# Memory attention with the rotary partner fetched by DMA between partitions

## The reference, cut to what matters

```python
qkv = xn @ w_qkv
q, k, v = jnp.split(qkv, 3, axis=-1)
rot = jnp.stack((-t2[..., 1], t2[..., 0]), axis=-1).reshape(t.shape)   # t2: t in pairs
roped = t * cos + rot * sin                                            # t: q and k
# per segment, with memory mem and norm z
sdpa = softmax(mask(roped_q @ roped_k.T * SCALE)) @ v
sq, sk = elu(q) + 1, elu(k) + 1
mem_out = (sq @ mem) / (sq @ z + 1e-6)
out = beta * mem_out + (1.0 - beta) * sdpa
prev_v = (sk @ mem) / (sk @ z)
mem = mem + sk.T @ (v - prev_v)
z = z + sk.sum(axis=2)
o = concat(out) @ w_out
```

## Time and profile before

| | |
|---|---|
| median of three runs | 2839.58 us |
| profiled execution, its own time | 2842.93 us |
| its span | 2840.8 us |
| TensorE busy in the whole span | 2095.6 us (74%) |
| VectorE | 1985.0 us (70%) |
| ScalarE | 1418.4 us (50%) |
| GpSimd | 1079.2 us (38%) |
| memory attention, about | 298 to 1130 us |
| its DMA traffic from 332 to 1130 us | 1 GB/s |

### The profile page before, as it was taken

The page is one execution under the profiler, slowest core; times in us unless marked ns, Lnnn a source line. Parts: engine busy times, 40 slices in busy tenths (PEclk is TensorE's granted clock), DMA queues, the critical chain, the costliest instruction groups (busy, mean ns, idle before and its releaser), DMA issues. The chain is left out here.

```text
span 2840.8 us, 87273 instructions
## 1 busy us (share of the span) xinstructions
PE 2095.6 (74%) x35326; PEld 1682.5 (59%) x35326; DVE 1985.0 (70%) x4767; ACT 1418.4 (50%) x2385; POOL 1079.2 (38%) x873
## 2 busy tenths in 40 slices
PE   3687599999999997679398947656666545558894
PEld 2576478888888876568278946433222233336794
DVE  5787577777777775779664433889999966757443
ACT  1555234444444442447364522468988754436452
POOL 3656334455554442556365621000000122206563
PEclk7789699999999998679699975765555577868997
DMA  4132200000000000023413220000000000012324
GB/s 109 45 103 83 80 2 0 0 0 0 0 0 0 0 0 3 31 83 93 147 45 91 73 88 0 0 0 1 1 0 0 0 1 1 0 36 70 88 77 114
DMA packets 95266, 104.00 MB, mean 37 GB/s; under 512 B 18936, under 2 KB 81000, under 8 KB 94464
## 3 DMA queue, kind: packets, MB, share of 16 engines
q1 hardware_dynamic: 74416, 64.12, 8.3%
q0 software_dynamic: 18176, 37.79, 3.9%
q10 hardware_dynamic: 2512, 0.02, 0.0%
HBM read 60.00 MB, written 46.20 MB: 37 GB/s over the span
## 5 line engine op out<-in xcount | busy, mean ns | idle before, releaser
L2472 POOL TENSOR_TENSOR bw_kT<-b_knT,b_head_of 128x768 f32<-128x768 f32 x40 | 58.5, 1494 | 650.7 <-SPq L2295 493.6
L2269 DVE CUSTOM_DVE_ANT_0 be_logs<-be_joint,be_logs 128x1024 f32<-128x1024 f32 x256 | 293.3, 1220 | 7.5 <-ACT be_logs L2242 7.5
L2242 ACT ACTIVATE be_logs<-be_joint,b_tiny 128x1024 f32<-128x1024 f32 x256 | 281.0, 1117 | 10.0 <-PE be_joint L2212 3.4
L2212 PE MATMUL be_joint<-be_partsT_k,be_partsT_q 64*128 64x512 f32 x512 | 195.4, 767 | 93.4 <-DVE be_sums L2269 89.9
L405 POOL DMA_INDIRECT d_pairs<-s_y_tile,s_x_tiles x156 | 178.6, 1145 | 119.4 <-DVE s_y_tile L1293 94.9
L1600 POOL TENSOR_TENSOR m_roped_q<-m_raw_q,m_cos 128x1024 f32<-128x1024 f32 x32 | 75.9, 2373 | 371.7 <-ACT m_raw_q L1536 371.7
L2212 PEld LDWEIGHTS be_joint<-be_partsT_k,be_partsT_q 64*128 64x128 f32 x512 | 72.0, 278 | 215.8 <-DVE be_sums L2269 211.3
L405 POOL DMA_INDIRECT d_pairs<-g_y_tile,g_x_tiles x156 | 153.9, 986 | 97.5 <-ACT g_y_tile L828 73.1
L332 POOL DMA_INDIRECT d_rows<-g_xn,g_slot x128 | 131.7, 1029 | 80.0 <-DVE g_slot L323 43.6
L332 POOL DMA_INDIRECT d_rows<-s_xn,s_slot x128 | 128.9, 1007 | 73.6 <-DVE s_slot L323 37.3
L1142 PE MATMUL s_ps_y<-s_down,s_a_tile 128*128 x1248 | 151.8, 275 | 0.0
(11 more groups left out here) (464 smaller groups left out, 6338.4 us busy)
## 6 DMA issues: line engine op xcount, KB each, us to landing
g_x_tiles<-d_rows SPq DMA_DIRECT2D x78, 132.0 KB, 2.1
s_x_tiles<-d_rows SPq DMA_DIRECT2D x78, 132.0 KB, 2.1
d_rows<-d_rows SPq DMA_DIRECT2D x32, 132.0 KB
g_shared<-d_pairs SPq DMA_DIRECT2D x8, 512.0 KB, 7.4
g_xn<-d_pairs SPq DMA_DIRECT2D x8, 512.0 KB, 7.5
s_up_raw<-L_ffn_We SPq DMA_DIRECT2D x16, 256.0 KB, 5.3
s_down<-L_ffn_We SPq DMA_DIRECT2D x16, 256.0 KB, 5.8
s_up_raw<-d_pairs SPq DMA_DIRECT2D x8, 512.0 KB, 7.5
```

What stands on the lines that cost most here:

```text
L2212: last = nc.tensor.matmul(joint_ps[k % DEPTH][:, a, :], partsT[0][rows, b, i * P:(i + 1) * P], partsT[1][rows, b, half * 512:(half + 1) * ...
L2242: nc.scalar.activation(logs[k % DEPTH][:, :, :], joint_ps[k % DEPTH][:, :, :], ACT.Ln, bias=A.tiny[:, :]).then_inc(s.log_ready, 1)
L2269: nc.vector.tensor_tensor_reduce(out=flat, in0=joint_ps[k % DEPTH][:, :, :].rearrange("p a j -> p (a j)"), in1=flat, scale=1.0, scalar=0.0 ...
L2472: last = nc.gpsimd.tensor_tensor(kT[:, h, :, :], A.knT[:, bass.ds(j * GROUP, KEYS), :], A.head_of[:, h:h + 1].unsqueeze(2).broadcast_to([P ...
```

## The change

The second set of fills goes, with `w_rot`. `front_spin` on VectorE now multiplies the same fill that gives `raw` by `signed_sin` (sin with the sign of the partition it is to leave from) into `spun`, after ScalarE has copied that half. SyncE then copies `spun` to `turned`, odd partitions to even ones and even to odd, in halves of 512 columns: eight transfers a tile, each of 64 partitions of 2 KB. GpSimd's products and sums are in halves too: all four products first, then the four sums, each of which waits for its transfers.

The orders change. k comes ahead of q everywhere. k's fills use banks 1 and 3 and q's banks 0 and 2; `project` uses bank 1 in place of a bank of `back_ps`. `scores(w)` moves from the end of tile `w - 1` to behind `recall_q` of tile `w`. VectorE begins a tile with `norm_1`, `back_u` and `back_o`, and the softmax follows in four parts around the two `back_mem`. Semaphores are split by q and k. The prologue fills k first, and TensorE no longer computes scores in it.

```diff
+            def swap(f, k):
+                spun_sem, moved, roped_sem = ((s.q_spun, s.q_moved, s.q_roped), (s.k_spun, s.k_moved, s.k_roped))[k]
+                for half in range(2):
+                    chunks = slice(4 * half, 4 * half + 4)
+                    wait_alone(sp, spun_sem, at(f, 2, half + 1), s.passed)
+                    wait(sp, roped_sem, at(f, 2, half - 1))
+                    sp.dma_start(turned[k][0::2, chunks, :], spun[k][1::2, chunks, :]).then_inc(moved[half], 16)
+                    sp.dma_start(turned[k][1::2, chunks, :], spun[k][0::2, chunks, :]).then_inc(moved[half], 16)
...
-            def fill_q(f, half):
-                if half == 0:
-                    pe.wait_ge(s.xnT_ready, f + 1)
+            def fill_k(f, half):
+                if half == 0:
+                    pe.wait_ge(s.xnT_ready, f + 1)
+                    wait(pe, s.scores_read, f)
+                fill(2 * half + 1, w_qkv, INNER + 512 * half, s.k_full)
+            def fill_q(f, half):
                 wait(pe, s.phik_copied, at(f, 2, half - 1))
                 fill(2 * half, w_qkv, 512 * half, s.q_full)
-                wait(pe, s.scores_read, f)
-                fill(2 * half + 1, w_rot, 512 * half, s.q_full)
...
             def recall_q(w, half):
-                wait_alone(pe, s.u_ready, at(w, 2, half + 1), s.passed)
+                if half == 0:
+                    pe.wait_ge(s.q_phi, w + 1)
+                wait_alone(pe, s.back_step, at(w, 8, 2 * half + 2), s.passed)
                 recall(phi_qT, half)
...
                 recall_q(w, 0)
-                if more:
-                    fill_q(w + 1, 0)
                 recall_q(w, 1)
-                if more:
-                    fill_q(w + 1, 1)
+                scores(w)
                 additions(w, 0)
                 if more:
                     fill_k(w + 1, 0)
+                    fill_k(w + 1, 1)
                 additions(w, 1)
                 if more:
-                    fill_k(w + 1, 1)
+                    fill_q(w + 1, 0)
+                    fill_q(w + 1, 1)
                 answers(w)
                 if more:
                     fill_v(w + 1)
-                project(w)
-                if more:
-                    scores(w + 1)
+                project(w, more)
...
+            def rope_moved(f, k):
+                cos_sem, moved, roped_sem = ((s.q_cos, s.q_moved, s.q_roped), (s.k_cos, s.k_moved, s.k_roped))[k]
+                for half in range(2):
+                    chunks = slice(4 * half, 4 * half + 4)
+                    pool.wait_ge(cos_sem, at(f, 2, half + 1))
+                    pool.wait_ge(moved[half], at(f, 32, 32))
+                    nc.gpsimd.tensor_tensor(roped[k][:, chunks, :], roped[k][:, chunks, :], turned[k][:, chunks, :], ALU.add).then_inc(roped_sem, 1)
...
+                for half in range(2):
+                    wait(dve, moved[half], 32 * f)
+                    dve.wait_ge(copied, at(f, 2, half + 1))
+                    nc.vector.tensor_tensor(spun[k][:, 4 * half:4 * half + 4, :], front_ps[2 * half + k][:, :].rearrange("p (k t) -> p k t", t=P),
+                                            wide(signed_sin).broadcast_to([P, 4, P]), ALU.mult).then_inc(spun_sem, 1)
...
-                softmax_1(w)
+                if norm:
+                    norm_1(w + 2)
                 back_u(w, 0)
                 back_u(w, 1)
-                softmax_2(w)
                 back_o(w, 0)
                 back_o(w, 1)
+                softmax_1(w)
+                back_mem(w, 0)
+                softmax_2(w)
+                back_mem(w, 1)
+                softmax_3(w)
+                softmax_4(w)
                 if more:
-                    front_rope(w + 1, 0)
-                back_mem(w, 0)
-                if norm:
-                    norm_1(w + 2)
-                back_mem(w, 1)
+                    front_spin(w + 1, 1)
+                    front_spin(w + 1, 0)
+                    front_phi(w + 1, 1)
                 if norm:
                     norm_2(w + 2)
                 if more:
                     front_phi(w + 1, 0)
-                    front_rope(w + 1, 1)
-                if more:
-                    front_phi(w + 1, 1)
                 back_x(w)
```

More of the change, by code:

```diff
@@ L1336, in memory_attention_stage @@
         beta_in, beta, over_beta, one_less_beta = (sb(n, [P, HEADS]) for n in ("beta_in", "beta", "over_beta", "one_less_beta"))
-        cos, sin = sb("cos", [P, P]), sb("sin", [P, P])
+        cos, sin, signed_sin = (sb(n, [P, P]) for n in ("cos", "sin", "signed_sin"))
+        odd, sign = sb("odd", [P, 1]), sb("sign", [P, 1])
         causal = sb("causal", [P, SEG])
@@ L1344, in memory_attention_stage @@
         raw = [sb(f"raw_{n}", [P, PAIRS, P]) for n in "qk"]
+        spun = [sb(f"spun_{n}", [P, PAIRS, P]) for n in "qk"]
         turned = [sb(f"turned_{n}", [P, PAIRS, P]) for n in "qk"]
@@ L1379, in _, with tile @@
             sp.wait_ge(s.loaded, 16 * (LOADS - 1))
+            def swap(f, k):
[6 more added lines that the diff above has]
+                    sp.dma_start(turned[k][1::2, chunks, :], spun[k][0::2, chunks, :]).then_inc(moved[half], 16)
+            def tile(w):
+                if not (isinstance(w, int) and w == TILES - 1):
+                    swap(w + 1, 1)
+                    swap(w + 1, 0)
+            swap(0, 1)
+            swap(0, 0)
+            in_tiles(sp, tile)
+            for half in range(2):
+                sp.wait_ge(s.k_moved[half], 32 * TILES)
+                sp.wait_ge(s.q_moved[half], 32 * TILES)
         @block.tensor
@@ L1424, in scores @@
             def scores(f):
-                wait_alone(pe, s.rope_done, at(f, 2, 2), s.passed)
+                wait(pe, s.x_done, f)
+                pe.wait_ge(s.q_roped, at(f, 2, 2))
+                wait_alone(pe, s.k_roped, at(f, 2, 2), s.passed)
                 for h in range(HEADS):
@@ L1481, in answers, with project @@
                 last.then_inc(s.back_full, 1)
-            def project(w):
+            def project(w, more):
+                if more:
+                    pe.wait_ge(s.k_copied, at(w + 1, 2, 1))
+                    pe.wait_ge(s.k_spun, at(w + 1, 2, 1))
+                else:
+                    pe.wait_ge(s.scores_read, w + 1)
                 pe.wait_ge(s.oT_ready, w + 1)
                 for k in range(PAIRS):
-                    last = nc.tensor.matmul(back_ps[:, 2, 0:D], oT[:, k, :], w_out[:, k, :], start=(k == 0), stop=(k == PAIRS - 1))
+                    last = nc.tensor.matmul(front_ps[1][:, 0:D], oT[:, k, :], w_out[:, k, :], start=(k == 0), stop=(k == PAIRS - 1))
                 last.then_inc(s.back_full, 1)
@@ L1507, in tile @@
                     fill_v(w + 1)
-                project(w)
-                if more:
-                    scores(w + 1)
+                project(w, more)
                 if more and not (isinstance(w, int) and w == TILES - 2):
                     turn_x(w + 2)
-            pe.wait_ge(s.set_up, 4)
+            pe.wait_ge(s.loaded, 16 * (LOADS - 1))
+            pe.wait_ge(s.set_up, 2)
             turn_x(0)
             for half in range(2):
+                fill_k(0, half)
+            for half in range(2):
                 fill_q(0, half)
-            for half in range(2):
-                fill_k(0, half)
             fill_v(0)
-            scores(0)
             turn_x(1)
@@ L1579, in _ @@
             copy_x(0)
-            front(0, 0)
-            front(0, 1)
+            for k in (1, 0):
+                copy_raw(0, k)
+                elu(0, k)
             copy_v(0)
@@ L1755, in _ @@
             dve.wait_ge(s.loaded, 16 * (LOADS - 1))
[L1756 to L1760 removed]
+            nc.vector.tensor_reduce(odd[:, :], c.ident[:, 1::2], AX.X, ALU.add).then_inc(s.sign_step, 1)
+            dve.wait_ge(s.sign_step, 1)
+            nc.vector.tensor_scalar(sign[:, :], odd[:, :], -2.0, 1.0, ALU.mult, ALU.add).then_inc(s.sign_step, 1)
+            dve.wait_ge(s.sign_step, 2)
+            nc.vector.tensor_scalar(signed_sin[:, :], sin[:, :], sign[:, 0:1], None, ALU.mult).then_inc(s.sign_step, 1)
+            dve.wait_ge(s.set_up, 2)
             nc.vector.reciprocal(over_beta[:, :], beta[:, :])
@@ L1765, in _ @@
                 norm_2(f)
-            front_rope(0, 0)
-            front_phi(0, 0)
-            front_rope(0, 1)
-            front_phi(0, 1)
+            dve.wait_ge(s.sign_step, 3)
+            for k in (1, 0):
+                front_spin(0, k)
+            for k in (1, 0):
+                front_phi(0, k)
             in_tiles(dve, tile)
```

95 lines of the change are left out of this document (45 added, 50 removed).

## The result

The changed kernel takes 2887.14 us (median of 4 runs, 2868.77 to 2888.43) against 2839.3 beside it: a ratio of 1.0155 (95%: 1.0113 to 1.0197), 48 us slower where 66 faster were forecast. The profiled execution has a span of 2886.5 us. In this document a ratio is taken over the executions within 1.5% of their kernel's fastest alone, and in pad64, pad32 and before_pad64 the traced execution is slower than that.

The account below looks back on a forecast made before the run. TensorE's order bounds today's tile; a loop through VectorE would set 21.6 us, plus 1.2 for clock drops: 22.8. Tiles -63, start -9, slower first and last tiles +5 give -67: 2773 us, range 2742 to 2822.

Parts of the forecast that it names:

- the list of bounds in "What sets the new period": Tile loop: TensorE's own work at most 19 us, a loop through VectorE and back 21.6 us; other dependencies checked as covered.
- the range of 2742 to 2822: Whole kernel: time range in us covering the forecast, the clock staying as before, and slow GpSimd halves.
- The clock: TensorE's `fill_v` and `project` after idle ahead of `answers`: drops in two of three tiles, 1.7 us each, +1.2 per tile.
- The tile at full clock: Loop from `recall_k` through VectorE to `answers` at 13.8 us, then 7.8 us of TensorE: 21.6 us against 24.24.
- The 0.5 us at the loop's turn: End of TensorE's tile, after `turn_x`: 0.5 us for the loop's turn, counted within TensorE's 7.8 us.
- TensorE's idle of 1.4 us ahead of `answers`: Between `fill_q`, ending at 12.3 us, and `answers` at 13.8: TensorE idles 1.4 us, released by VectorE.
- the wait for GpSimd: VectorE's part of the loop: waits for GpSimd of 0.4 us, placed at `softmax_3`'s product.
- GpSimd in halves: GpSimd's products and sums over 512 columns: 1.28 us each, some at 2, eight making 11 us per tile.
- The rival at 1.5 us: GpSimd halves take about 1.5 us and hold VectorE: 22.6 + 1.2 = 23.8 us per tile, 2804 us; chance 0.16.
- The transfers: Eight SP transfers a tile: landing near 2.1 us, 0.4 us of SP each, 3.2 per tile, hidden.
- The slower rival, late transfers: Late landing delays q's sum, `scores` and `softmax_1`: 2853 us at 8 us landing, 2881 at 9; chance 0.09.
- The start: Before and in the first tile: no wait for the rotation, -7 us to first `recall_k`, -2 in the tile, -9 together.

Follow-up runs that it names:

- pad64: Changed kernel with 64 already met waits on TensorE right ahead of its loop over tiles: 2809 us against 2841 for the kernel before, ratio 0.9814.
- pad32: Changed kernel with 32 already met waits ahead of TensorE's loop: 2914 us against 2957 for the kernel before, ratio 0.9747; repeated, 2940 us, 0.9951.
- before_pad64: Kernel before the change with 64 more instructions at the start of TensorE's block: 2904 us against 2839 unpadded, ratio 1.0147.
- before_pad128: Kernel before the change with 128 already met waits ahead of TensorE's loop: 3217 us against 2841 unpadded, ratio 1.1313.
- pad12: Changed kernel with 12 already met waits ahead of TensorE's loop: 2895 us against 2943 for the kernel before, ratio 0.9863.
- pad128: Changed kernel with 128 already met waits ahead of TensorE's loop: 2837 us against 2841 for the kernel before, no ratio.
- early64: Changed kernel with 64 more instructions at the start of TensorE's block: 2929 us against 2957 for the kernel before, ratio 0.9902.
- pad244: Changed kernel with 244 more instructions at the start of TensorE's block: 2882 us against 2839 for the kernel before, ratio 1.0173.
- still: Changed kernel without the eight transfers a tile, GpSimd adding `spun` itself: 2818 us against 2841 for the kernel before, ratio 0.9926.
- twice_still: Changed kernel with 64 early TensorE instructions, q's second half filled twice and no transfers: 2856 us against 2943 for the kernel before, ratio 0.9698.

## Why the prediction was wrong

- **The step that failed** is the list of bounds in "What sets the new period". It names TensorE's own work, VectorE's loop, GpSimd, the transfers and the clock, and takes TensorE's instructions to be there when they are due. What the runs show in its place: an instruction stream that stops in nine tiles, at +12.8 us each, 115 us. No rival held it, so the range of 2742 to 2822 missed. Moving the loop in both kernels shows the cause: pad64 takes the fetches away from the changed kernel (0.981), before_pad128 gives them to the other (1.131).
- **The clock** was mis-sized, on both sides. The short drop costs 1.7 us, as taken; the long one costs 2.8 (23.9 against 21.1), since the clock stays at 0.50 for over 6 us, through `fill_v` and into `project` (pad64, 617 to 623 us), and no term held it. In two of three tiles a drop was forecast; eight of the 19 ordinary tiles of the changed kernel have one, eight of 22 in pad12's good rhythm, and nearly every tile in the traces of pad64, pad128, pad32 and early64. The change with its loop at a clean place thus measures 0.5 to 2.5% faster by the ratios (pad12, pad32, pad64, early64) and 0.2 to 1.6% by the medians of all executions (pad128 too), with tiles of about 24.2 us in all traces but pad12's, where the forecast was 2.3% and 22.8 us. pad12's trace, mostly in the good rhythm, has 22.6 us. That 2887 - 115 = 2772 equals the forecast is partly chance: the ordinary tiles of the changed kernel took 22.0 us and not 22.8 (31 x 0.8 = -25), the first and last ones 11 more than taken, the start gained 5 less, and 6 were lost behind the stage. That a long tile breaks the rhythm of the drops is likely and not shown: six of the nine are followed by a tile of 21.1 us, but in pad244 twelve tiles of 23.9 end in one of 21.1 with no long tile between.
- **The tile at full clock** was right: 21.1 us against 21.6, with `answers` at 13.8 us. The 0.5 us at the loop's turn isn't there: `turn_x` runs from 617.50 to 617.77 and `recall_k` begins at 617.71. TensorE's idle of 1.4 us ahead of `answers` measured 0.95. I put the wait for GpSimd at `softmax_3`'s product, where 0.4 us were taken; it stands in `softmax_2`'s, 0.46 against 0.17.
- **GpSimd in halves** was right for the products (1.28 us taken, 1.281 measured); k's sums take 1.60 on average, where some at 2 were expected, and the loop doesn't wait for them. The rival at 1.5 us, with a tile of 22.6 at full clock, fell. The cost beside VectorE was right in kind; `norm_2`'s 1.34 us lies off the loop.
- **The transfers** were right: 2.0 us to landing (2.1 taken). SP takes 0.47 to 0.60 us for each (0.4 taken), which nothing waits for. The slower rival, late transfers, fell with still and twice_still. The result was slower, but not by it.
- **The start** gained 4.3 us to the first sum into X, not 9.

## What to carry to other kernels

When an edit changes how many instructions an engine issues inside or ahead of a loop of more than a thousand, look at q8's packets and at idle time put down to "issue" inside one run of products before judging the edit: the same loop was 13% slower or not at all by 128 waits placed ahead of it. Price an idle wait on TensorE by the clock it loses downstream, not by its own length: filling 1 us of idle gave back 1.9 us per tile where each tile had had a drop. And time one edit at two or three places of the loop, in several executions each, before saying what it is worth: the place alone moved it from 1.4 to 1.6% above the kernel before (on one chip level with it) to 0.5 to 2.5% below, and at one place executions differed by 2 to 3%.

## What was not expected of the hardware

- A loop of TensorE that fits is kept: 0 packets in some 28 turns. One that is read again takes nine packets of 16 KB, some 4 us apart, and 32 to 38 us where 21 to 26 are usual. With loops of almost one length (6.08 and 6.31 blocks) the place alone decides.
- The reading again can be partial: in 4 to 9 of 28 turns, and in nine and then seven in executions of one program.
- A drop of the clock can lock to the tile: 26 of pad64's 28 tiles have a long one, while `fill_v` runs. It can also set in or end within one execution (pad12, pad244).
